# Four layers of a graph network on one core: layer 0 begins ahead of the Laplacian, its layer norm moves to GpSimd, the eigenvector chain and its products are placed anew

## The chip, the core and the metric

The kernel runs on one core of one Trainium2 chip. Time is device time in microseconds (us), the median of three runs. The engines are PE (TensorE), DVE (VectorE), ACT (ScalarE), POOL (GpSimd) and SP, which issues the transfers. Each works through its own program in order; they meet through semaphores.

## The reference

x is 128 x 64 x 128 floats (8192 rows of 128), `adj` a weighted 64 x 64 adjacency matrix. Four layers follow one another, each of this form:

```python
h = jnp.maximum(_layernorm(x, axis=-1), 0.0)
x = x + _L0_gnn_ref(h, adj, ...)   # then _L1_, _L2_, _L3_ in the same way
```

Layer 0 multiplies by the normalised adjacency matrix, then by W1 (to 256), batch norm over all rows, relu, W2 (back to 128) and batch norm again. Layer 1 is two graph convolutions and then four LSTMs over windows of 1, 2, 3 and 4 nodes, one after the other:

```python
h = jax.nn.relu(jnp.einsum('ts,bsh->bth', adj, x @ Wg0 + bg0))
h = jax.nn.relu(jnp.einsum('ts,bsh->bth', adj, h @ Wg1 + bg1))
for p in range(1, MAX_SKIP + 1):
    wins = h[:, :nw * p, :].reshape(Bv * nw, p, Hd)
    last = _lstm_last(Wih[p - 1], Whh[p - 1], bih[p - 1], bhh[p - 1], wins)
    h = h.at[:, idx, :].set(last.reshape(Bv, nw, Hd))
```

Layer 2 needs the eigenvectors of the normalised Laplacian, a 64 x 64 matrix that depends on `adj` alone:

```python
_, U = jnp.linalg.eigh(L_norm)
agg = jnp.einsum('mn,bnd->bmd', U.T, features)
h = jax.nn.relu(agg @ W1 + b1)
out = h @ W2 + b2
return jnp.einsum('nm,bmd->bnd', U, out)
```

Layer 3 is three products with `adj * adj`, each with a weight matrix. The kernel's output is x after all four.

## The kernel before

x lies in SBUF (tile X) as 16 chunks of 512 columns (4 tiles of 128); chunks come in ITER = 4 groups of NK = 4. A 64-node graph fills half the partitions, so 128 x 128 matrices made of two equal blocks (BDHT, BDP, BDR and their like) do the aggregation.

**Start.** DVE builds these matrices from `adj` one `step` after the other, first BDA and BDAT, then BDHT for layer 0, then the Laplacian LS and the matrix S that is to be reduced (lines 1271 to 1284). PE waits for "S" before its first layer-0 instruction.

**Layer 0, REFLECTED = 28 steps.** The first L0_FIRST = 19 steps pass the 16 chunks through statistics, norm, aggregation (`agg`) and W1 (`w1`), one stage a step; the other 9 do W2, two chunks a step. Beside each step stands one Householder reflection of S (`reflection_beside_l0`, lines 1335 to 1381): DVE writes NI (line 1344), PE returns a row (`row_product`), DVE copies the norm (1350), POOL takes a root (1125), DVE forms vcol (1361), PE returns a product with S (`av_product`), DVE updates S (1379, 1381). DVE's layer-0 work is a generator (`beside`, `l0_first`), from which the reflection takes an instruction wherever it would wait. The layer norm of a chunk is 4 bn_stats (line 1825), 4 bn_aggr (1832) and a shift (1841) on DVE, and on POOL a scaling (1133) and a power (1135); ACT applies it (953). In step r = 2 DVE makes the matrices of layer 1 (lines 1923 to 1928).

**The LSTM, four times (i = 0 to 3).** PE runs products of 512, 336 or 256 columns for the rounds of the four LSTMs, ACT the gates, POOL the element-wise products (line 1156). Beside iteration i the first half of layer 1 for group i + 1 is done ("tasks", the table TASKS gives the round, set and half in which each product stands). The eigenvector chain goes on beside it: the remaining 34 reflections (one `av_product` each), a grid of shifts counted by sign changes in two rounds (tile Z, lines 1529 to 1590), the twist (`both_ways`), a scan over Fq, five products on EV that correct the vectors. Their products on PE are "small": `eigen_products` yields the distance to the next in units of PE work (PACE_AV, PACE_GRID and so on), `spend` counts PE's work and sends the small product when it is due. On DVE layer 1's instructions are put between those of the chain (`beside_l1`) by a model of when PE will be where (DVE_STEP, PASS, LN_STEP, SLOWED). These two orders are fixed when the program is written; at run time an engine that reaches an instruction whose semaphore is not there waits, and all behind it with it.

**The end of the LSTM.** After the eigenvectors are done (semaphore value "all", line 1749) DVE does the layer norms' statistics for the next layers (`last_stats`: 16 x 2 bn_stats, aggregations, roots by Newton steps). In the last iteration DVE, not POOL, does the element-wise products from round 6 on (line 2050). Then follow layers 2 and 3.

Line 513 is the helper for all matrix products, line 531 a transpose of the start.

## Time and profile before

| | |
|---|---|
| median of 3 runs | 926.91 us (926.87 to 927.29) |
| the profiled execution, its time | 924.75 us |
| its span | 923.0 us |
| mean granted clock of PE | 0.972 |
| PE busy | 810.1 us (88%) |
| DVE busy | 579.1 us (63%) |
| ACT busy | 507.4 us (55%) |
| POOL busy | 311.1 us (34%) |

The chain that ended last lies on PE for 50% of the span, on DVE for 16%, on ACT for 7%. In time the program is: start to 14 us, first half of layer 0 to about 117, second half to about 160, LSTM to about 633, layers 2 and 3 to 923.

A timeline row is: start us, duration us, engine, line, operation, out<-in with shapes, xcount, and in brackets the idle time of the engine just before it and what ended that. PEld is PE's loading of a weight matrix. A window row is: start:end, length, then the busy time of PE, PEld, DVE, ACT and POOL with the number of instructions, the granted clock (1.0 is 2.4 GHz, 0.5 is 1.2 GHz), the share of the DMA engines and GB/s; a window row of PE alone has one busy time. A group row by form is: line, engine, operation, xcount, busy us, mean ns, idle us before. A row of waits is: engine, what it wrote, its line, what it waited for, total us, number, longest us.

### The profile page before, as it was taken

The page shows a single profiled execution, that of the slowest core. Times are in us where ns is not written, and L with a number is a line of the kernel's source. Part 1 is how long each engine was busy: PE and PEld are TensorE (multiplying, and loading weights), DVE is VectorE, ACT ScalarE, POOL GpSimd, SP SyncE. Part 2 cuts the span into 40 slices and gives each one's busy share as a digit, 9 for nine tenths or more (in the row PEclk, how much of TensorE's full clock was granted, in tenths as well). Part 3 has the DMA queues.
Part 4 walks back from the last instruction along what each step waited for, and adds up shares of the span by engine and source line. Part 5 has one row for each costly group of instructions (what it writes and reads, how often), then busy time and mean ns, then how long its engine had stood idle before and what let it go on. Part 6 is the DMA issues. An engine that isn't in the chain of part 4 may idle for free.

```text
span 923.0 us, 15727 instructions
## 1 busy us (share of the span) xinstructions
PE 810.1 (88%) x5323; PEld 522.7 (57%) x5323; DVE 579.1 (63%) x3092; ACT 507.4 (55%) x958; POOL 311.1 (34%) x365
## 2 busy tenths in 40 slices
PE   2787598799999988998689879988899999999998
PEld 1444343654578545684356634566656756757746
DVE  5899878689777996689794986944830530510101
ACT  1566486565755727557276464585564464443531
POOL 1233211266545735557456465600230040010000
PEclk9999989699999989999899999999999999999999
DMA  8000000000000000000000000000000100100101
GB/s 359 1 1 1 1 0 1 1 0 1 0 1 1 1 0 2 1 1 0 1 0 1 1 0 1 1 1 2 2 1 1 48 2 1 48 1 1 49 0 46
DMA packets 3408, 13.48 MB, mean 15 GB/s; under 512 B 512, under 2 KB 512, under 8 KB 2688
## 3 DMA queue, kind: packets, MB, share of 16 engines
q1 hardware_dynamic: 3328, 12.48, 3.4%
q8 instruction: 42, 0.69, 0.3%
q14 instruction: 38, 0.31, 0.1%
HBM read 8.28 MB, written 4.19 MB: 14 GB/s over the span
## 4 chain that ended last, share of the span: by engine, by line
PE 50%; DVE 16%; ACT 7%; issue 2%; POOL 2%; DVEq 0%; ACTq 0%
PE PS L513 49%; ACT BIG L1041 2%; ACT T L1007 2%; POOL BIG L1156 2%; DVE X L2032 1%; ACT T L953 1%; DVE Fq L1628 1%; DVE seg L1629 1%; DVE stats L1825 1%; ACT BIG L1065 1%; PE PS L699 1%; DVE stats L1804 1%; DVE PS L1522 1%; DVE PS L1524 1%; DVE Z L1529 1%
## 5 line engine op out<-in xcount | busy, mean ns | idle before, releaser
L513 PE MATMUL PS<-BIG,wts 128*128 128x512 f32 (+2 forms) x952 | 339.8, 499 | 10.4 <-ACT BIG L1041 8.0
L1156 POOL TENSOR_TENSOR BIG<-BIG 128x256 f32<-128x256 f32 (+2 forms) x220 | 211.5, 969 | 159.5 <-ACT BIG L1041 93.9
L513 PEld LDWEIGHTS PS<-BIG,wts 128*128 128x128 f32 x952 | 176.5, 192 | 132.9 <-issue 95.0
L1041 ACT ACTIVATE BIG<-PS,lbias 128x256 f32<-128x256 f32 (+2 forms) x312 | 162.2, 560 | 106.3 <-PE PS L513 104.3
L513 PE MATMUL PS<-H,wts 128*128 128x256 f32 (+2 forms) x312 | 113.3, 488 | 11.7 <-POOL H L1156 5.4
L945 ACT ACTIVATE BIG<-PS 128x1024 f32<-128x1024 f32 x64 | 64.8, 1023 | 85.4 <-PE PS L513 85.0
L513 PE MATMUL PS<-T,wts 128*128 128x512 f32 x192 | 100.9, 647 | 1.8 <-ACT T L945 1.6
L2077 DVE COPY T<-PS 128x256 f32<-128x256 f32 x32 | 12.0, 417 | 136.0 <-PE PS L513 136.0
L945 ACT ACTIVATE T<-PS 128x512 f32<-128x512 f32 (+1 forms) x96 | 48.3, 523 | 78.0 <-PE PS L513 77.7
L953 ACT ACTIVATE T<-X,shift,rstd 128x128 f32<-128x128 f32 x192 | 78.6, 483 | 18.2 <-DVE shift L1841 18.2
L513 PEld LDWEIGHTS PS<-H,wts 128*128 128x128 f32 x312 | 56.3, 193 | 45.2 <-issue 18.8
L2032 DVE TENSOR_TENSOR X<-X,PS 128x512 f32<-128x512 f32 x64 | 41.8, 679 | 63.0 <-PE PS L513 56.3
L1133 POOL TENSOR_SCALAR rstd<-mv 128x4 f32<-128x4 f32 x44 | 10.0, 228 | 208.6 <-DVE mv L1832 208.6
L1065 ACT ACTIVATE BIG<-BIG 128x512 f32<-128x512 f32 (+2 forms) x88 | 44.8, 510 | 51.7 <-POOL BIG L1156 50.1
L513 PE MATMUL PS<-wts,T 128*128 128x128 f32 (+1 forms) x384 | 61.9, 315 | 0.6 <-DVE T L2077 0.4
L513 PEld LDWEIGHTS PS<-wts,T 128*128 128x128 f32 x384 | 55.9, 194 | 8.0 <-issue 3.0
L513 PEld LDWEIGHTS PS<-wts,BIG 128*128 128x128 f32 x512 | 57.8, 192 | 1.9 <-issue 1.9
L513 PE MATMUL PS<-wts,BIG 128*128 128x128 f32 x512 | 57.8, 275 | 0.0
L513 PEld LDWEIGHTS PS<-T,wts 128*128 128x128 f32 x192 | 34.2, 197 | 32.9 <-issue 25.0
L1135 POOL TENSOR_TENSOR rstd<-rstd,cst 128x4 f32<-128x4 f32 x44 | 45.7, 1038 | 3.7
L1125 POOL TENSOR_TENSOR sc<-sc,cst 128x1 f32<-128x1 f32 x28 | 15.3, 548 | 93.4 <-DVE sc L1350 93.4
L1825 DVE BATCH_NORM_STATS2 stats<-X 128x6 f32<-128x128 f32 x208 | 46.6, 278 | 0.3
(319 smaller groups left out, 1136.5 us busy)
## 6 DMA issues: line engine op xcount, KB each, us to landing
X<-x_in SPq DMA_DIRECT2D x4, 1024.0 KB, 16.2
out<-X SPq DMA_DIRECT2D x16, 256.0 KB, 2.3
wts<-w_in SPq DMA_DIRECT2D x1, 3542.0 KB, 13.2
cst<-cst_in SPq DMA_DIRECT2D x1, 419.0 KB, 3.3
AA<-adj_in SPq DMA_DIRECT2D x2, 16.0 KB, 2.0
```

Source lines behind the costliest of these rows:

```text
L513: return nc.tensor.matmul(o, l, r, start=start, stop=stop)
L945: nc.scalar.activation(dst, src, fn, **kw).then_inc(act_done[k], 1)
L953: j = nc.scalar.activation(to[:, k, t * P:(t + 1) * P], X[:, a:a + P], ACT.Relu, bias=shifted[:, k, t:t + 1], scale=scale[:, k, t:t + 1])
L1007: j = nc.scalar.activation(T0[:, k, t * P:(t + 1) * P], X[:, a:a + P], ACT.Relu, bias=shift[:, k, t:t + 1], scale=rstd[:, k, t:t + 1])
L1041: nc.scalar.activation(LB[:, q, {"i": I_, "g": G_, "f": F_, "o": O_}[g], 0:n], PS[:, 3 * q + rank[q] % 3, 0:n], ACT.Tanh if g == "g" else ...
L1065: nc.scalar.activation(LB[:, q, I_, 0:n], LB[:, q, CELL, 0:n], ACT.Tanh).then_inc(act_set[q], 1)
L1125: return nc.gpsimd.tensor_tensor(o, ap, mh[:, 0:1] if e is None else e, ALU.pow)
L1135: nc.gpsimd.tensor_tensor(to[:, k, :], to[:, k, :], mh[:, 0:TPC], ALU.pow).then_inc(pool_done[k], 1)
L1156: nc.gpsimd.tensor_tensor(out, a, b, op).then_inc(pool_set[q], 1)
L1825: j = v.bn_stats(stats[:, k, t, :], X[:, a:a + P])
L2032: v.tensor_tensor(x, x, src, ALU.add).then_inc(dve_done[k], 1)
L2077: v.tensor_copy(*graph_half(k, 1, to, side)).then_inc(dve_done[k], 1)
```

## The change

1. Layer 0 starts before the Laplacian. PE waits for "hat" (BDHT) only. Steps are now counted by n, L0_STEPS = 28; the Laplacian stands on DVE in step 1, reflections begin at step FIRST_REFLECTED = 3. So 25 reflections are beside layer 0 and 37 beside the LSTM.
2. Layer 0's layer norm is bn_stats on DVE and then ten small operations on POOL (`whole_layer_norm`), which also write the shift; ACT waits for POOL.
3. The matrices of layer 1 and the LSTM's biases are made in step BIASES_AT = 23, in the second half.
4. Row and av products take 128 rows of S instead of 64.
5. The two long passes over Z become four quarters each (is_lt now against a tile of zeros), the reduction a tree of adds; instructions of layer 1 can stand between all of them.
6. New paces and new times in the model, and new places of `turn` and `turn_h` in TASKS.
7. `last_stats` is merged into the eigenvector chain; it begins 24 units after the last group's second aggregation.

```diff
-A_DVE = Steps(BEGUN, LN)
+A_DVE = Steps(BEGUN, ["stats"])
-A_POOL = Steps(BEGUN, LNP)
+A_POOL = Steps(BEGUN, WHOLE_LN)
...
+L0_STEPS = L0_FIRST + L0_SECOND
+FIRST_REFLECTED = 3
+REFLECTED = L0_STEPS - FIRST_REFLECTED
+BIASES_AT = L0_FIRST + 4
-PACE_AV = 6.7
-PACE_GRID = [47.0, 43.0]
-PACE_TWIST = 40.0
+PACE_AV = 5.9
+PACE_GRID = [49.0, 41.5]
+PACE_TWIST = 33.0
-SMALL = 0.5
+SMALL = 0.45
-SLOWED = 1.08
+SLOWED = 1.04
-PASS = 2.1
-LN_STEP = 0.5
+PASS = [0.45, 0.45, 0.45]
+QUARTER = NODES // 4
+LN_STEP = 0.42
+NORM_BESIDE, NORM_LASTS, LAST_NORMS = 1.4, 20.0, 24.0
...
-                mm(eb(0)[:, 0:NODES + 1 - k], S[0:NODES, k:k + 1].broadcast_to((NODES, P)),
-                   NI[0:NODES, k + 1:NODES + 2]).then_inc(hh_row, 1)
+                mm(eb(0)[:, 0:NODES + 1 - k], S[:, k:k + 1].broadcast_to((P, P)), NI[:, k + 1:NODES + 2]).then_inc(hh_row, 1)
...
-            pe.wait_ge(prep_dve, PREP["S"])
+            pe.wait_ge(prep_dve, PREP["hat"])
+            for n in range(L0_STEPS):
+                r, m = n - FIRST_REFLECTED, n - L0_FIRST
+                if n == 3:
+                    pe.wait_ge(prep_dve, PREP["S"])
+                if r >= 0:
+                    row_product(r)
...
+                if pace is not None and beside_norm():
+                    pace += NORM_BESIDE
...
+            def whole_layer_norm(i, k):
+                pool.wait_ge(dve_done[k], A_DVE.at(i, "stats"))
+                g.tensor_tensor(apart, even, odd, ALU.subtract).then_inc(pool_done[k], 1)
+                g.tensor_tensor(mean2, even, odd, ALU.add).then_inc(pool_done[k], 1)
+                g.tensor_tensor(m2, m2_even, m2_odd, ALU.add).then_inc(pool_done[k], 1)
+                see("apart")
+                g.tensor_tensor(between, apart, apart, ALU.mult).then_inc(pool_done[k], 1)
+                see("sum")
+                g.tensor_scalar(m2, m2, 1.0 / P, EPS, ALU.mult, ALU.add).then_inc(pool_done[k], 1)
+                g.tensor_scalar(mean2, mean2, -0.5, None, ALU.mult).then_inc(pool_done[k], 1)
+                see("square")
+                g.tensor_scalar(between, between, 0.25, None, ALU.mult).then_inc(pool_done[k], 1)
+                see("between")
+                g.tensor_tensor(var, m2, between, ALU.add).then_inc(pool_done[k], 1)
+                see("var")
+                g.tensor_tensor(rstd[:, k, :], var, mh[:, 0:TPC], ALU.pow).then_inc(pool_done[k], 1)
+                see("rstd")
+                g.tensor_tensor(shift[:, k, :], mean2, rstd[:, k, :], ALU.mult).then_inc(pool_done[k], 1)
...
-                    gop(v.tensor_scalar(Z[:, 0:NODES, :], Z[:, 0:NODES, :], 0.0, None, ALU.is_lt))
-                    busy(3 * PASS)
-                    gop(v.tensor_tensor(Z[:, 0:NODES - 1, :], Z[:, 0:NODES - 1, :], Z[:, 1:NODES, :], ALU.not_equal))
+                    for a in range(0, NODES, QUARTER):
+                        busy(PASS[0])
+                        gop(v.tensor_tensor(Z[:, a:a + QUARTER, :], Z[:, a:a + QUARTER, :], zeros, ALU.is_lt))
+                        gsync()
+                    for a in range(0, NODES, QUARTER):
+                        b = min(a + QUARTER, NODES - 1)
+                        busy(PASS[1])
+                        gop(v.tensor_tensor(Z[:, a:b, :], Z[:, a:b, :], Z[:, a + 1:b + 1, :], ALU.not_equal))
+                        gsync()
...
-                    gop(v.tensor_reduce(cn, Z[:, 0:NODES, :].rearrange("p i m -> p m i"), AX, ALU.add))
+                    while half > 2:
+                        half //= 2
+                        for a in range(0, half, QUARTER):
+                            b = min(a + QUARTER, half)
+                            busy(PASS[2] * (b - a) / QUARTER)
+                            gop(v.tensor_tensor(Z[:, a:b, :], Z[:, a:b, :], Z[:, half + a:half + b, :], ALU.add))
+                            gsync()
+                    gop(v.tensor_tensor(cn, Z[:, 0, :], Z[:, 1, :], ALU.add))
...
+            for n in range(L0_STEPS):
+                if n == 1:
+                    laplacian()
+                if n == BIASES_AT:
...
-                    at = [there[ITER - 2, NK - 1, "turn_h"]]
+                    at = [there[ITER - 1, NK - 1, "agg2"] + LAST_NORMS]
...
-                        yield from behind
-                        yield from last_stats()
+                        yield from merged(last_stats(), behind)
```

Three places at which instructions stand otherwise. First, DVE's program at the passes over Z in the first round of the grid (L1804 are layer 1's bn_stats). Before:

```order
L1560 TENSOR_SCALAR Z<-Z 128x2048 [waits grid_ops]
L1563 TENSOR_TENSOR Z<-Z 128x2016 [waits grid_ops]
L1804 BN_STATS stats<-X 128x6
L1565 SCALAR_TENSOR_TENSOR Z<-xg,PS 128x32 [waits grid_ops,dve_done2]
L1804 BN_STATS stats<-X 128x6
L1567 TENSOR_REDUCE counts<-Z 128x32 [waits grid_ops]
L1804 BN_STATS stats<-X 128x6
L1573 TENSOR_SCALAR tmp<-cst,counts 128x128 [waits grid_ops]
```

After (L1615 is the comparison with zero, L1620 the one with the neighbour, L1841 to L1853 roots of layer 1's norm, L2110 the add into X):

```order
L1615 TENSOR_TENSOR Z<-Z,zero 128x512 [waits grid_ops]
L1841 TENSOR_TENSOR lnv<-lnv 128x16 [waits ln_ops]
L1615 TENSOR_TENSOR Z<-Z,zero 128x512 [waits grid_ops]
L2110 TENSOR_TENSOR X<-X,PS 128x512 [waits pe_done2]
L1615 TENSOR_TENSOR Z<-Z,zero 128x512 [waits grid_ops]
L1844 TENSOR_TENSOR lnv<-lnv 128x16 [waits ln_ops]
L1615 TENSOR_TENSOR Z<-Z,zero 128x512 [waits grid_ops]
L1847 SCALAR_TENSOR_TENSOR lnv<-lnv 128x16 [waits ln_ops]
L1620 TENSOR_TENSOR Z<-Z 128x512 [waits grid_ops]
L1850 SCALAR_TENSOR_TENSOR lnv<-lnv 128x16 [waits ln_ops]
L1620 TENSOR_TENSOR Z<-Z 128x512 [waits grid_ops]
L1853 TENSOR_SCALAR rstd<-lnv 128x16 [waits ln_ops]
```

A pass is now four instructions, and layer 1's stand between them.

Second, PE's program around the second product of the grid, PS<-sc,cst, in the third iteration of the LSTM (BIG,wts are gates of the LSTM). Before:

```order
L513 MATMUL PS<-BIG,wts 128x256 [waits act_set1,pool_set1]
L513 MATMUL PS<-BIG,wts 128x256 [waits act_set1] x2
L513 MATMUL PS<-wts,T 128x128 [waits act_done2,act_done1]
L513 MATMUL PS<-wts,T 128x128 x3
L513 MATMUL PS<-sc,cst 128x1 [waits grid_cnt]
L513 MATMUL PS<-BIG,wts 128x256 [waits act_set0] x3
```

After:

```order
L525 MATMUL PS<-BIG,wts 128x256 [waits pool_set0]
L525 MATMUL PS<-BIG,wts 128x256 x2
L525 MATMUL PS<-BIG,wts 128x256 [waits act_set0]
L525 MATMUL PS<-BIG,wts 128x256
L525 MATMUL PS<-sc,cst 128x1 [waits grid_cnt]
L525 MATMUL PS<-BDR,T 128x128 [waits act_done2,dve_done1]
L525 MATMUL PS<-BDR,T 128x128 x3
```

The product now stands ahead of the second aggregation (agg2, BDR,T) of chunk 2, where it stood among the g1 products (PS<-wts,T) of the same iteration.

Third, DVE's program from the twist (both_ways) to the scan (Fq). Before:

```order
L1650 TENSOR_SCALAR both_ways<-Fq 64x64 [waits prep_dve]
L1651 TENSOR_TENSOR Fq<-Fq,Tdir 128x64 [waits prep_dve]
L1652 TENSOR_SCALAR Fq<-Fq 128x64 [waits prep_dve]
L1653 COPY both_ways<-Fq 64x64 [waits prep_dve]
L1656 TENSOR_TENSOR Fq<-PS,Fq 128x64 [waits prep_pe,prep_dve]
L1657 TENSOR_TENSOR Fq<-Fq 128x64 [waits prep_dve]
L1658 TENSOR_REDUCE sc<-Fq 128x1 [waits prep_dve]
```

After (L2066 are bn_stats of `last_stats`):

```order
L1716 TENSOR_TENSOR Fq<-Fq,Tdir 128x64 [waits prep_dve]
L1717 TENSOR_SCALAR Fq<-Fq 128x64 [waits prep_dve]
L1718 COPY both_ways<-Fq 64x64 [waits prep_dve]
L2066 BN_STATS stats<-X 128x6 [waits prep_dve]
L2066 BN_STATS stats<-X 128x6 x2
L2066 BN_STATS stats<-X 128x6 [waits dve_done1]
L2066 BN_STATS stats<-X 128x6 x2
L1721 TENSOR_TENSOR Fq<-PS,Fq 128x64 [waits prep_pe]
L2066 BN_STATS stats<-X 128x6
L1722 TENSOR_TENSOR Fq<-Fq 128x64 [waits prep_dve]
L2066 BN_STATS stats<-X 128x6 [waits dve_done2]
```

What stood behind the whole chain before stands inside it.

## Rows read from the trace of the kernel before

**Rows 1.** Windows, all engines, 245 to 340 (LSTM stage): busy us, granted clock.

```profile
245.00:340.00 95.00, 91.86 (x393) 61.15 (x391) 76.84 (x529) 53.94 (x104) 54.09 (x60) 0.98 0.00 1
```

**Rows 2.** Timeline of layer 0, DVE: start, duration, engine, line, operation.

```profile
64.29 0.23 DVE L1344 TENSOR_SCALAR NI<-cst,S 128x2 f32<-128x2 f32 x1
...
69.55 0.23 DVE L1344 TENSOR_SCALAR NI<-cst,S 128x2 f32<-128x2 f32 x1
...
101.03 0.23 DVE L1344 TENSOR_SCALAR NI<-cst,S 128x2 f32<-128x2 f32 x1
...
105.81 0.23 DVE L1344 TENSOR_SCALAR NI<-cst,S 128x2 f32<-128x2 f32 x1
```

**Rows 3.** Timeline of the start, DVE.

```profile
10.79 0.35 DVE L1269 TENSOR_SCALAR BDHT<-PS,col 128x128 f32<-128x128 f32 x1 [0.64 <-PE PS L531]
...
14.47 0.23 DVE L1344 TENSOR_SCALAR NI<-cst,S 128x2 f32<-128x2 f32 x1
...
23.70 0.28 DVE L1923 TENSOR_SCALAR tmp<-PS 128x128 f32<-128x128 f32 x1
...
26.25 0.23 DVE L1344 TENSOR_SCALAR NI<-cst,S 128x2 f32<-128x2 f32 x1
...
37.74 0.23 DVE L1344 TENSOR_SCALAR NI<-cst,S 128x2 f32<-128x2 f32 x1
```

**Rows 4.** Timeline of the second half of layer 0, PE's weight load.

```profile
132.95 0.18 PEld L513 LDWEIGHTS PS<-NI,S 64*128 64x128 f32 x1 [0.87 <-DVE NI L1344]
```

**Rows 5.** Groups by form, POOL: xcount | busy us, mean ns | idle before.

```profile
L1156 POOL TENSOR_TENSOR BIG<-BIG 128x256 f32<-128x256 f32 x82 | 58.9, 726 | 48.6 <-ACT BIG L1041 34.2 <-ACT BIG L1065 12.9
...
L1135 POOL TENSOR_TENSOR rstd<-rstd,cst 128x4 f32<-128x4 f32 x44 | 45.7, 1038 | 3.7
...
L1133 POOL TENSOR_SCALAR rstd<-mv 128x4 f32<-128x4 f32 x44 | 10.0, 228 | 208.6 <-DVE mv L1832 208.6
```

**Rows 6.** Waits of PE in 160 to 500: total, times, longest, in us.

```profile
PE PS L699 <- DVE X L2032: 7.8, 1, 7.8
PE PS L513 <- DVE S L1443: 7.0, 5, 2.2
```

**Rows 7.** Windows of PE at the lower clock (four stretches).

```profile
445.30:452.10 6.80, 3.80 (x8) 0.50 0.00 0
...
sum 17.00, PE 14.00; mean PE 3.50
```

**Rows 8.** Timeline of DVE beside the LSTM: one reflection's step, one root's operation.

```profile
225.44 1.07 DVE L1779 TENSOR_TENSOR lnv<-lnv 128x16 f32<-128x16 f32 x1
...
227.26 0.17 DVE L1779 TENSOR_TENSOR lnv<-lnv 128x16 f32<-128x16 f32 x1
...
231.93 0.27 DVE L1443 TENSOR_SCALAR S<-S,sc 128x1 f32<-128x1 f32 x1
...
236.85 0.27 DVE L1443 TENSOR_SCALAR S<-S,sc 128x1 f32<-128x1 f32 x1
```

**Rows 9.** Groups by form, DVE: the two long passes over Z.

```profile
L1567 DVE TENSOR_REDUCE counts<-Z 128x32 f32<-128x2048 f32 x2 | 7.3, 3673 | 0.0
...
L1563 DVE TENSOR_TENSOR Z<-Z 128x2016 f32<-128x2016 f32 x2 | 6.0, 3017 | 0.1
```

**Rows 10.** Timeline from the grid's second product to the twist.

```profile
505.57 0.28 PE L513 MATMUL PS<-sc,cst 128*128 128x1 f32 x2
...
521.70 1.16 PE L513 MATMUL PS<-BDR,T 128*128 128x128 f32 x8 [1.01 <-DVE T L1970]
...
550.10 0.23 DVE L1656 TENSOR_TENSOR Fq<-PS,Fq 128x64 f32<-128x64 f32 x1 [1.85 <-PE PS L513]
```

**Rows 11.** Timeline of the eigenvectors' end and DVE's first LSTM product.

```profile
578.75 0.33 PE L513 MATMUL PS<-EV,cst 64*64 64x64 f32 x2
...
586.76 0.28 DVE L1741 TENSOR_TENSOR EV<-EV,cst 64x128 f32<-64x128 f32 x1
...
600.06 0.92 DVE L2050 TENSOR_TENSOR BIG<-BIG 128x336 f32<-128x336 f32 x2
```

More of the change, by code:

```diff
@@ L174 @@
                    lambda i: of(i + 1, "norm3", "mix1T") * (i + 1 < ITER))
[L175 removed]
+D_DVE = two_layers(C_DVE.end, of(0, "half", "add_h") + of(1, "half") + of(0, "o", "add", *LN3)
                    + of(1, "o", "add") + of(0, "half3"),
@@ L675, in send, with beside_norm @@
                 clock[0] += SMALL
+                if pace is not None and beside_norm():
+                    pace += NORM_BESIDE
                 due[0] = None if pace is None else max(due[0], clock[0] - 1.0) + pace
+            def beside_norm():
+                return any((j, 1, "turn") in there and clock[0] < there.get((j, NK - 1, "turn"), clock[0]) + NORM_LASTS
+                           for j in range(1, ITER))
             def spend(us, i=None, k=None, name=None):
@@ L964, in _ @@
                     i, k = divmod(n - 1, NK)
-                    norm_tiles(i, k, "norm", A_DVE.at(i, "shift"), A_PE.start(i))
+                    norm_tiles(i, k, "norm", A_POOL.at(i, "shift"), A_PE.start(i), by=pool_done)
                 if is_chunk(n - 2):
@@ L1864, in l0_first @@
                         dve.wait_ge(act_done[k], A_ACT.at(i - 1, "norm"))
-                    yield from stats_of(i, k, A_DVE)
+                    for t in range(TPC):
+                        a = i * SG + k * CH + t * P
+                        j = v.bn_stats(stats[:, k, t, :], X[:, a:a + P])
+                        if t == TPC - 1:
+                            j.then_inc(dve_done[k], 1)
+                        yield
+                for _ in range(AFTER_STATS):
+                    yield
                 if is_chunk(n - 3):
```

144 lines of the change are left out of this document (78 added, 66 removed).

## The prediction

> **What bounds the kernel now.** I read the busy times of the stages first, then the waits of PE, then the timelines at the places that the change touches. Beside the LSTM (160 to 633 us) PE is the engine that everything else waits for: 91.86 of 95 us busy between 245 and 340 [rows 1]. There DVE's eigenvector chain costs something only where PE reaches one of its small products before DVE has delivered, or where DVE is late for an add: 7.8 us once before an add into X, 7.0 us in five waits for a reflection's S column, the longest 2.2 [rows 6]. Layer 0, before that, is a loop of DVE and PE around the reflection: a step takes 5.26 us with a layer norm in it (64.29 to 69.55) and 4.78 without one (101.03 to 105.81) [rows 2]. At the end of the LSTM the last rounds' products are DVE's own; the first starts at 600.06, only after the eigenvector chain and all of `last_stats`, so this chain sets the stage's end [rows 11]. Layers 2 and 3, from 633 on, are not touched.
>
> The sum is made against the profiled execution (924.75 us), which is 2.16 below the median of the runs (926.91).
>
> **Start of layer 0.** Before, BDHT ends at 11.14, the Laplacian follows, and reflection 0 starts at 14.47; reflections 0 to 3 then run beside a pipeline that is only filling, and reflection 4 starts at 37.74 [rows 3]. After, stats(0) come at 11.1 (-3.4), the six LSTM matrix operations (23.70 to 26.25, 2.55 us [rows 3]) are gone from the third step (-2.5), and three of the steps have no reflection. What fills the pipe instead is POOL's longer layer norm, ACT's norm, and PE's aggregation and w1: some 3 us longer than from stats to shift on DVE, but without the waits of three loops of about 4.8 us each [rows 2]. I take -1.1 for the two together (between +3 and -5). Start: -3.4 - 2.5 - 1.1 = **-7.0** (range -3 to -10).
>
> **Steps with a layer norm.** Four aggregations and the shift leave DVE in 12 steps. The step can lose between nothing (they stood in waits) and the 0.48 us by which a step with a layer norm is longer [rows 2]; the four stats stay, so I take a third, 0.17: **-2.0**. POOL now has ten small operations per chunk. Three TENSOR_SCALARs are 0.228 each, the pow 1.04 [rows 5]. The six small adds and products on 128x4 are not in the trace: at most the pow's 1.04, at least what 726 ns for 256 columns leaves, about 0.15. I take 0.25, nearest to the 0.228 row, and 0.07 between dependent ones: 0.7 + 1.0 + 1.5 + 0.7 = 3.9 us, with the reflection's own root (0.6) under 5.1, so POOL just fits the step.
>
> **LSTM matrices in the second half.** Those 2.55 us now stand in a loop in which PE waits 0.87 us for DVE's NI each step [rows 4], so they lengthen it: **+2.5** (0 if ACT hides them). Products over 128 rows instead of 64: PE's time goes by columns, 0. Layer 0 in all: -6.5.
>
> **Beside the LSTM, until the grid's second product.** The 7.8 and about 6 of the 7.0 us [rows 6] go, since the adds no longer stand behind the two long passes (3.67 and 3.02 us each [rows 9]) and the pauses near the norms are longer: -13.8. After each of those stalls PE ran at clock 0.50, that is 1.2 GHz; four such stretches, 17.0 us in which it was busy 14.0 [rows 7]. That is up to 7.0 lost; -5.0, as new stalls bring some back. New stalls: 37 reflections instead of 34 now stand closer (5.9 against 6.7 in the planner's units). A reflection's step without layer-1 work needs 4.92 us of DVE (231.93 to 236.85 [rows 8]); going through the 36 steps with the layer-1 instructions that the order puts between them (0 to 5.7 us a step, weighted 0.85), against 6.4 us of PE work on average and 4.9 at least, DVE is late in ten of them, by 0.3 to 1.4: +7.0. Around the first grid product the quarters and the add tree take as much as the passes they replace: +0.7. Together -13.8 - 5.0 + 7.7 = -11.1. In the new order the grid's second product stands right before the second aggregation (BDR,T) of chunk 2, which PE reached at 521.70 before [rows 10]; so it comes at 510.6, in before's time without layer 0's shift, and not at 505.57.
>
> **From there to DVE's LSTM products.** Before: 505.57 to 578.75, 73.2 us, to the last product on EV [rows 10, 11]. The twist's product is sent 7 units earlier, so its 1.85 us wait [rows 10] shrinks to 0.5: -1.35. Inside the scan DVE now has 9 stats, 16 aggregations, 8 root operations and an add: 33 by 0.17 [rows 8] and 0.5 for the add, +6.2 (at 0.10 each 3.8, at the disturbed 1.07 far more), in a stretch in which PE leaves it no wait. Between the EV products seven more: +1.3. The tail: 578.75 to 587.04 as before, 8.3, roots between 2.0, the four copies 1.3: 11.6 where it was 21.3 (to 600.06). Half clock in the new stalls +0.7. So 510.6 + 73.2 - 1.35 + 6.2 + 1.3 + 11.6 + 0.7 = 602.2 against 600.06: **+2.2**. The large saving before and the large saving of `last_stats` behind meet a chain that begins 5 us later and carries what was taken out behind it.
>
> Sum: -6.5 + 2.2 = -4.3, so the profiled execution at 920.4 and the median at **922.5**.
>
> **A rule weighed.** The same root operation on two SBUF inputs took 0.17 us at 227.26 and 1.07 at 225.44 [rows 8], with POOL in a long LSTM product at the second. The Trainium skill's "GPSIMD Engine Reference", Specifications, says that GpSimd's SBUF interfaces are shared with VectorE, with contention for DVE instructions that have two SBUF inputs. By that rule the trace agrees, and it speaks against this change: is_lt over Z had one input and gets a second (the zeros), and each long pass becomes pieces that can each wait for POOL. By the rule the sum would be rival E's; without it, mine.
>
> **Rivals.**
> A, faster. DVE keeps pace with the closer reflections and the scan's additions fall into its waits: no 7.0 and no 6.2, so 909.4; half of that 916. For it: DVE was busy only 76.8 of 95 us [rows 1]. Against it: the waits of PE for S at a looser pace [rows 6].
> B, slower. DVE bounds the reflections: the step needs 5.2 instead of 4.92 and layer-1 work counts in full. The same walk then gives 13.8 us of stalls instead of 7.0: 929.3. It decides from a need of about 5.2 a step; the disturbed 1.07 us in rows 8 speaks for it.
> C, slower. POOL bounds layer 0: if a small add takes over 0.34 us (at 0.45: 0.7 + 1.04 + 2.7 + 0.7 + 0.6 = 5.8 a step against 5.1), 13 steps by 0.7: +9, 931.5.
> D, the start does not do what its order says: ACT, POOL and a PE that is slow while cold fill the pipe as late as before, half of the 7.0 stays: 926.
> E, slower than my case. The pieces of the passes over Z, with two inputs each, wait for POOL's products as the operation at 225.44 did: some 15 pieces in the first round, half of which meet one and wait about 0.4 us (half of 1.07 less 0.17), in a stretch without slack: +3, 925.6. In the second round DVE has slack.
>
> **How the numbers follow.** My case 0.45 (own range 918 to 926), A 0.20, B 0.12, C 0.08, D 0.08, E 0.07. What a measurement of this kernel can tell from no change is about 0.2%, 1.85 us: faster is below 925.05, slower above 928.8. Faster: 0.40 of mine, 0.20 of A, 0.02 of D and E: 0.62. Same: 0.05 + 0.11 = 0.16. Slower: B, C and the upper ends of D and E, 0.22. The range reaches to half of A and to C: 912 to 931.
>
> **What would show it.** Layer 0: reflection 1 of the new count (the fifth step) at 30.7 in place of 37.74; steps of 5.1 with a layer norm and one of about 7.2 in the second half; POOL's ten operations in 3.9 us. Beside the LSTM: no wait before an add longer than 2 us, ten or so waits for S of 0.3 to 1.4, the grid's second product near 504 (510.6 - 6.5). DVE's first LSTM product near 596. The forecast is wrong if the reflections' waits sum to under 2 or over 12 us, if POOL's layer norm takes over 4.5, or if DVE's first LSTM product comes before 590 or after 600.

## The result, and the profile after

The changed kernel takes 898.35 us (median of 4 runs, 896.06 to 899.2) against 926.89 before: ratio 0.9688, 95% interval 0.967 to 0.9706. That is 28.5 us faster; 4.4 were forecast, and 898.35 lies outside the range of 912 to 931. The profiled execution has a span of 896.5 us, 26.5 less than before. All medians and ratios are of executions in the fast state; one execution, of e5, took 2819 us and is left out.

I lay the two traces side by side at the same matrix products, those that multiply BIG or H with a weight matrix (PS<-BIG,wts and PS<-H,wts). Both traces have 1264 of them; the first thousand or so are the LSTM's, the last ones lie in layers 2 and 3. The n-th of them starts so much earlier after the change:

```
n            0      270    330    510    570    600    780    840    900    1260
before    192.8    313.6  353.4  422.5  464.9  481.4  553.3  584.9  603.8  900.5
after     183.2    297.6  329.4  396.7  428.7  449.1  516.6  559.5  578.2  874.1
earlier     9.6     16.1   24.0   25.8   36.2   32.2   36.7   25.5   25.6   26.5
```

Three things are to be read from it. Up to the LSTM's first product it is 9.6 us. Beside the LSTM PE gains another 27, in part steadily, in part at the places where it waited before. And 11 of them are lost again between n = 780 and 840, that is from 517 to 560 us. The 9.6 is a reading of one execution: in e18, the same kernel profiled again, the first product starts at 180.8 and not at 183.2, so single profiles do not tell 2 us in layer 0 apart.

The start and the steps of layer 0, DVE, against [rows 2, 3] (the fifth step starts at 29.75, later ones are at 50.52 and 55.65, two of the second half at 142.85 and 147.16):

```profile
10.55 0.35 DVE L1316 TENSOR_SCALAR BDHT<-PS,col 128x128 f32<-128x128 f32 x1 [0.64 <-PE PS L543]
10.93 0.87 DVE L1928 BATCH_NORM_STATS2 stats<-X 128x6 f32<-128x128 f32 x4
...
16.98 0.22 DVE L1395 TENSOR_SCALAR NI<-cst,S 128x2 f32<-128x2 f32 x1
...
29.75 0.23 DVE L1395 TENSOR_SCALAR NI<-cst,S 128x2 f32<-128x2 f32 x1
```

```profile
50.52 0.23 DVE L1395 TENSOR_SCALAR NI<-cst,S 128x2 f32<-128x2 f32 x1
55.65 0.23 DVE L1395 TENSOR_SCALAR NI<-cst,S 128x2 f32<-128x2 f32 x1
```

```profile
142.85 0.23 DVE L1395 TENSOR_SCALAR NI<-cst,S 128x2 f32<-128x2 f32 x1
147.16 0.23 DVE L1395 TENSOR_SCALAR NI<-cst,S 128x2 f32<-128x2 f32 x1
```

A step of the first half takes 5.13 us (5.26 before), one of the second half 4.31 (4.63 before):

```profile
128.04 0.23 DVE L1344 TENSOR_SCALAR NI<-cst,S 128x2 f32<-128x2 f32 x1
132.67 0.23 DVE L1344 TENSOR_SCALAR NI<-cst,S 128x2 f32<-128x2 f32 x1
```

The last reflection beside layer 0 starts at 147.16, before at 155.76. The layer norm on POOL, by groups (xcount | busy us, mean ns | idle before), against [rows 5]:

```profile
L1180 POOL TENSOR_TENSOR rstd<-lnp,cst 128x4 f32<-128x4 f32 x16 | 16.6, 1039 | 1.3
...
L1174 POOL TENSOR_SCALAR lnp<-lnp 128x4 f32<-128x4 f32 x16 | 3.7, 228 | 1.3
...
L1169 POOL TENSOR_TENSOR lnp<-stats 128x4 f32<-128x4 f32 x16 | 3.3, 205 | 0.0
```

A small add takes 0.205 us (0.25 were assumed), and the ten operations of one chunk last from 47.33 to 50.44, 3.1 us, not 3.9. Between 30 and 110 us DVE waits for POOL once, for 0.5 us, so POOL does not bound the step.

Now the part beside the LSTM. These are windows of all engines over the same 480 products of the LSTM, first of before, then of after (length, busy PE, PEld, DVE, ACT, POOL, granted clock):

```profile
193.00:414.00 221.00, 208.99 (x863) 135.32 (x863) 178.34 (x1223) 132.75 (x261) 121.58 (x128) 0.98 0.00 1
```

```profile
183.20:387.90 204.70, 195.49 (x870) 133.49 (x869) 182.40 (x1284) 132.52 (x261) 122.48 (x129) 1.00 0.00 1
```

PE is idle for 9.2 us in place of 12.0, so hardly less. But it is *busy* for 13.5 us less, with the same work and a few more small products. Part of it is the clock: after has no stretch at the lower clock there, before had three of 3.4 us each, in which up to half the time is lost, by my estimate up to 5 us. The rest is in the timeline of PE around one reflection's small products, first before, then after:

```profile
223.11 1.02 PE L513 MATMUL PS<-BIG,wts 128*128 128x512 f32 x2
224.06 0.40 PE L513 MATMUL PS<-S,cst 64*128 64x27 f32 x2
224.31 0.38 PE L513 MATMUL PS<-S,vcol 64*128 64x29 f32 x2
224.62 1.13 PE L513 MATMUL PS<-BIG,wts 128*128 128x512 f32 x2
```

```profile
191.35 1.45 PE L525 MATMUL PS<-BIG,wts 128*128 128x512 f32 x3
192.63 0.38 PE L525 MATMUL PS<-S,cst 128*128 128x33 f32 x2
192.85 0.39 PE L525 MATMUL PS<-S,vcol 128*128 128x35 f32 x2
193.07 0.63 PE L714 MATMUL PS<-cst,T 128*128 128x128 f32 x4
```

Before, the last product of 512 columns starts at 223.54 and the small ones 0.52 us later; then it is 0.31 from the second pair to the next gate product. After, the same distances are 0.43 (192.20 to 192.63) and 0.22. From the large product before to the product behind the small ones it is 1.08 before and 0.87 after, and over all reflections beside the LSTM the median of this distance falls from 0.93 to 0.65 us. The small products of after even have more columns (33 and 35 for 27 and 29); what could make them shorter is "128*128" in place of "64*128", the number of rows. e5 and e6 test it.

The waits of PE in after, 150 to 610 us (total, times, longest), against [rows 6]:

```profile
PE PS L525 <- DVE both_ways L1718: 8.8, 1, 8.8
PE PS L525 <- ACT BIG L1061: 8.4, 11, 1.4
PE PS L525 <- ACT T L1027: 6.3, 2, 4.6
PE PS L525 <- POOL H L1205: 5.6, 4, 2.6
PE PS L525 <- DVE S L1416: 3.7, 1, 3.7
...
PE PS L719 <- DVE X L2110: 2.3, 2, 2.1
```

No wait for a reflection beside the LSTM is left (line 1494 is absent), and the wait of 7.8 before the add is 2.1. In their place stands one of 8.8 us for `both_ways`. (The wait of 3.7 for L1416 belongs to the last reflection beside layer 0, and before had it too.) And DVE in 160 to 640 us waited for PE in the reflections, first before, then after:

```profile
DVE sc L1456 <- PE PS L513: 38.7, 22, 4.8
```

```profile
DVE sc L1507 <- PE PS L525: 20.2, 20, 4.6
```

So DVE had 38.7 us of slack in the reflections before, and the closer pace used half of it.

The lower clock, against [rows 7]: three stretches, one behind the wait at 430, one that begins at 525.3, inside the wait of 523 to 531, and one behind the wait at 546 us.

```profile
433.00:437.00 4.00, 4.00 (x10) 2.29 (x9) 4.00 (x7) 1.62 (x3) 3.06 (x2) 0.57 0.01 2
526.00:536.00 10.00, 4.50 (x11) 2.72 (x12) 9.45 (x45) 0.00 (x0) 0.26 (x1) 0.52 0.00 0
548.50:552.00 3.50, 3.44 (x6) 1.40 (x6) 1.58 (x11) 0.69 (x1) 0.69 (x1) 0.60 0.00 0
```

The eigenvector chain from the grid's second product, against [rows 10, 11]:

```profile
489.49 0.28 PE L525 MATMUL PS<-sc,cst 128*128 128x1 f32 x2
```

```profile
531.50 0.79 PE L525 MATMUL PS<-both_ways,cst 128*128 128x128 f32 x2 [8.79 <-DVE both_ways L1718]
...
548.32 0.24 PE L590 MATMUL PS<-cst,Fq 64*64 64x64 f32 x1 [1.88 <-DVE Fq L1757]
```

```profile
563.98 0.33 PE L525 MATMUL PS<-EV,cst 64*64 64x64 f32 x2
...
573.30 0.23 DVE L1814 COPY BDUT<-PS 64x64 f32<-64x64 f32 x1
573.57 0.93 DVE L2128 TENSOR_TENSOR BIG<-BIG 128x336 f32<-128x336 f32 x2
```

DVE's first LSTM product starts at 573.57, 26.5 us earlier, and that is the whole gain of the span: 322.9 us follow it in both kernels.

### The profile page after: what moved, and what is told of

The parts are those of the page before. It is cut to its first block, busy times and chain, and to the rows that moved or that the text cites. A ratio compares the mean times of both kernels' runs of the same rounds, so it can differ in the third digit from the quotient of the medians.

```text
span 896.5 us, 15860 instructions
## 1 busy us (share of the span) xinstructions
PE 792.7 (88%) x5323; PEld 520.6 (58%) x5323; DVE 577.7 (64%) x3091; ACT 505.6 (56%) x958; POOL 330.9 (37%) x490
## 4 chain that ended last, share of the span: by engine, by line
PE 57%; DVE 26%; ACT 8%; POOL 5%; issue 3%; DMA 0%; DVEq 0%; SPq 0%; ACTq 0%; POOLq 0%
PE PS L525 56%; POOL BIG L1205 2%; ACT BIG L1061 2%; ACT T L1027 2%; DVE ST L1914 2%; DVE Fq L1693 1%; DVE seg L1694 1%; ACT T L973 1%; DVE X L2110 1%; DVE PS L1575 1%; DVE PS L1577 1%; DVE Z L1582 1%; DVE Z L1579 1%; ACT BIG L1085 1%; POOL sc L1145 1%
## 5 line engine op out<-in xcount | busy, mean ns | idle before, releaser
L525 PE MATMUL PS<-H,wts 128*128 128x256 f32 (+2 forms) x312 | 111.3, 485 | 10.8 <-POOL H L1205 5.6
L525 PE MATMUL PS<-T,wts 128*128 128x512 f32 x192 | 104.8, 670 | 2.9 <-ACT T L965 2.5
L973 ACT ACTIVATE T<-X,shift,rstd 128x128 f32<-128x128 f32 x192 | 78.6, 483 | 10.3 <-POOL shift L1182 9.5
L2110 DVE TENSOR_TENSOR X<-X,PS 128x512 f32<-128x512 f32 x64 | 41.9, 680 | 61.7 <-PE PS L525 56.1
L1153 POOL TENSOR_SCALAR rstd<-mv 128x4 f32<-128x4 f32 x28 | 6.4, 228 | 190.6 <-DVE mv L1897 190.5
L525 PEld LDWEIGHTS PS<-T,wts 128*128 128x128 f32 x192 | 36.0, 208 | 34.8 <-issue 28.1
L525 PEld LDWEIGHTS PS<-S,vcol 128*128 128x128 f32 x124 | 20.8, 201 | 30.8 <-DVE S L1416 26.9
L525 PE MATMUL PS<-S,vcol 128*128 128x64 f32 (+61 forms) x124 | 24.2, 275 | 13.2 <-DVE S L1416 13.1
```

The source lines that it names most:

```text
L525: return nc.tensor.matmul(o, l, r, start=start, stop=stop)
L973: j = nc.scalar.activation(to[:, k, t * P:(t + 1) * P], X[:, a:a + P], ACT.Relu, bias=shifted[:, k, t:t + 1], scale=scale[:, k, t:t + 1])
L2110: v.tensor_tensor(x, x, src, ALU.add).then_inc(dve_done[k], 1)
```

## The experiments

Each is timed beside the kernel before on the same chip. The changed kernel itself was 898.35 in the first comparison and 896.58 in e18; differences under 2 us from it are not told apart by these runs. Diffs named e1 to e3, e5, e7 to e12, e14 to e17 are against the changed kernel; e4, e6 and e13 against the kernel before.

**e1, the twist's product 4 units later.**

```diff
-PACE_TWIST = 33.0
+PACE_TWIST = 37.0
```

> The changed kernel with PACE_TWIST 37 in place of 33: PE sends the twist's product 4 units of its work later. In the changed kernel PE waits 8.8 us for both_ways. Theory 1 (from the grid's second product on DVE's own chain sets when its LSTM products can begin, and PE's wait is only the visible end of it): the wait falls from 8.8 to about 4.5, DVE's first LSTM product stays near 573.6, time 897 to 899, no change. Theory 2 (PE's progress sets the end, each of its waits is paid in full): the time falls by the 4 us of the wait, to about 894. Rival to both (the later product delays the scan behind it, as DVE already waits for it): slower by up to 3, 901.

904.19 us, ratio 0.9759 [0.9742, 0.9777]: slower than the changed kernel by 5.8. The wait for both_ways fell to 3.8, and still nothing was won, for the later places of all small products behind the twist made the chain end 4.7 us later (last product on EV at 568.64 in place of 563.98), and DVE's first LSTM product at 578.58. DVE now waited 3.0 and 2.7 us for PE among the EV products. Theories 1 and 2 both failed. The rival (slower by up to 3) had the direction and was too small: behind the twist the places in PE's program can delay the chain's end.

**e2, reflections 5.3 apart.**

```diff
-PACE_AV = 5.9
+PACE_AV = 5.3
```

> The changed kernel with PACE_AV 5.3 in place of 5.9: the 37 reflections stand closer, some 22 us of PE work in all, and the grid, twist and scan come as much earlier. Theory 1 (DVE's chain sets the start of its LSTM products): the chain ends 15 to 20 us earlier, PE's own progress then sets the end; as PE still waits 8.8 for both_ways, the gain is only the 1 to 3 us by which DVE's first LSTM product is late against its gates: 895 to 898. Theory of the prediction (a reflection needs 4.92 plus its layer-1 instructions, so new waits of 15 us or more appear at the reflections): slower, 905 to 913. If DVE's need is lower (mean about 5.0): waits for the S column under 4 us in sum.

907.57 us, 0.9789 [0.9764, 0.9815]. The waits of PE in 183 to 396 us:

```profile
PE PS L525 <- DVE S L1494: 9.8, 11, 1.8
```

So 5.3 is too close, by the prediction's kind of wait. The time lies in the 905 to 913 that its theory gave, but the waits are of less than its size (it would have given 15 or more). The chain came earlier and helped nothing. The shortest steps of DVE here are 4.72 and 4.73 us, below the 4.92 on which the prediction built.

**e3, reflections 5.6 apart, the twist's product 9 units later.**

```diff
-PACE_AV = 5.9
+PACE_AV = 5.6
-PACE_TWIST = 33.0
+PACE_TWIST = 42.0
```

> The changed kernel with PACE_AV 5.6 and PACE_TWIST 42: reflections 11 units of PE work earlier in all, the twist's product 9 later against the grid's. Theory 1: the chain begins 11 us earlier and ends about 10 earlier, the wait of 8.8 for both_ways is gone and the clock's fall behind it: faster by 8 to 11, 888 to 891. Theory 2 (waits are paid in full, whatever the chain does): the same 8 to 11. Theory of the prediction (reflections bound by DVE): 4 to 7 us of new waits at the reflections, 893 to 896.

899.56 us, 0.9714 [0.9678, 0.9749]: no better, and outside what all three theories said. The wait for both_ways is gone, but PE waits 5.4 us for S, 4.4 once before the add, and more for ACT and POOL. What DVE doesn't deliver earlier, PE can't gain by asking in another place.

**e4, the kernel before with the closer pace alone.**

```diff
-PACE_AV = 6.7
+PACE_AV = 5.9
```

> The kernel before with PACE_AV 5.9 in place of 6.7 and nothing else: one part of the change alone. Theory 1 (what counts is when DVE's LSTM products can begin and PE's waits): the chain ends some 25 us earlier, last_stats fall before the last rounds, DVE's first LSTM product is no longer late (2.3 us before), but the wait of 7.8 before the add and the clock's fall behind it stay or move: 921 to 926. Chain theory (the chain's length sets the end of the stage): 905 or less. Theory of the prediction (new waits at the reflections): slower, 928 to 934.

920.71 us, 0.9936 [0.9918, 0.9954], 5.7 us faster. The eight waits for S sum to 6.2 us (before: five, 7.0); on the first 300 products it is 6.1 us *later* than before, as the prediction thought of the pace; it gains at the add, where the 7.8 are gone (the long passes fall elsewhere), and at the end of the chain. Theory 1 (921 to 926) came nearest.

**e5 and e6, the rows of the small products.** e5: on the changed kernel 64 rows again; e6: on the kernel before 128 rows and nothing else (row_product, old_row and av_product alike). One of e5's three lines:

```diff
-                mm(eb(2)[:, 0:NODES - k], vcol[:, 0:1].broadcast_to((P, P)), S[:, k + 1:NODES + 1]).then_inc(hh_av, 1)
+                mm(eb(2)[:, 0:NODES - k], vcol[0:NODES, 0:1].broadcast_to((NODES, P)), S[0:NODES, k + 1:NODES + 1]).then_inc(hh_av, 1)
```

> The changed kernel with its row, old-row and av products on 64 rows again; all else stays. Theory M (a product on 64 rows between products on 128 makes PE empty and change over: around a reflection's small products PE needs 1.07 us from one gate product to the next before and 0.79 after, 0.28 a reflection): +0.28 x 37 = 10 beside the LSTM, +0.3 in each of the 6 second-half steps and 0.1 to 0.2 in the first half's, 12 to 16 in all, 910 to 914. Theory of the prediction (PE's time goes by columns, rows cost nothing): 898 to 899. Theory 1 (DVE's chain sets the LSTM products' start): under 5, since PE has 8.8 us of waiting for both_ways to give: 900 to 903.

> The kernel before with these products on 128 rows and nothing else. Theory M: 34 x 0.28 = 9.5 beside the LSTM and 3 to 5 in layer 0, where both products are in the loop of DVE and PE: 912 to 915, less if the wait before the add grows by what PE is earlier. Theory of the prediction: 926 to 927.

e5: 910.48 us, 0.981 [0.979, 0.983], slower than the changed kernel by 12.1. e6: 915.85 us, 0.9875 [0.9857, 0.9893], faster than before by 11.1. e5 lies in theory M's range, e6 0.9 us above it, and the prediction's nothing is refuted. In e5 PE is 4.1 us later when the LSTM begins and 10.8 after 480 products; its window over these products against that of after above:

```profile
187.20:398.80 211.60, 204.87 (x871) 134.39 (x870) 183.24 (x1285) 132.52 (x261) 122.58 (x130) 1.00 0.00 1
```

PE is busy 9.4 us more for the same work, at the same clock. The median distance around the small products is 0.92 in e5 and 0.65 in e6. In layer 0 the rows count in the second half alone: its steps are 4.63 in e5 and 4.31 in e6 (4.31 and 4.63 without the edit), those of the first half stay at 5.12 and 5.27.

The weight loads (PEld) show where the time goes. The same reflection, first after, then e5; the large product ahead of it starts at 187.03 and 190.83, the last small one at 187.71 and 191.71:

```profile
187.15 0.49 PEld L525 LDWEIGHTS PS<-S,cst 128*128 128x128 f32 x2 [0.36 <-DVE S L1494]
187.46 0.31 PE L525 MATMUL PS<-S,cst 128*128 128x34 f32 x2
...
187.79 0.30 PEld L525 LDWEIGHTS PS<-BIG,wts 128*128 128x128 f32 x2
187.82 0.68 PE L525 MATMUL PS<-BIG,wts 128*128 128x512 f32 x1
```

```profile
191.35 0.29 PEld L525 LDWEIGHTS PS<-S,cst 64*128 64x128 f32 x2 [0.76 <-DVE S L1494]
191.35 0.41 PE L525 MATMUL PS<-S,cst 64*128 64x34 f32 x2
...
191.91 0.30 PEld L525 LDWEIGHTS PS<-BIG,wts 128*128 128x128 f32 x2
191.91 0.70 PE L525 MATMUL PS<-BIG,wts 128*128 128x512 f32 x1
```

With 128 rows the first load for the small products begins 0.12 us after the large product does, 0.31 ahead of its own product. With 64 rows it begins only together with its own product, 0.52 after the large one. That is so at every reflection beside the LSTM: in before and e5 all 34 and 37 loads begin within 0.002 us of their product, in after and e6 33 of 37 and 28 of 34 begin at least 0.1 ahead. Start to start, the extra 0.28 us of a reflection is 0.09 before the first small product, 0.10 between its two passes and 0.09 behind the last one.

**e7, last_stats behind the chain again.**

```diff
-                        yield from merged(last_stats(), behind)
+                        yield from behind
+                        yield from last_stats()
```

> The changed kernel with last_stats behind the eigenvector chain again. Theory 1 (DVE's chain ends at 573.5, about when the gates of round 6 are there, so what is put behind it counts in full): DVE's first LSTM product 9 to 12 us later, less 2 to 3 because the scan and the EV products are lighter: 905 to 908. Rival (ACT and POOL have a store of work there): 898 to 900.

904.16 us, 0.9749 [0.9734, 0.9764]: 5.8 slower, a little less than theory 1 said (905 to 908) and far from its rival.

**e8, layer 0's norm on DVE again.**

```diff
-A_DVE = Steps(BEGUN, ["stats"])
+A_DVE = Steps(BEGUN, LN)
-A_POOL = Steps(BEGUN, WHOLE_LN)
+A_POOL = Steps(BEGUN, LNP)
...
-                    whole_layer_norm(n // NK, n % NK)
+                    layer_norm_roots(n // NK, n % NK, A_POOL, A_DVE)
```

> The changed kernel with layer 0's norm as before: 4 aggregations and the shift on DVE, two operations on POOL. Theory of the prediction: +0.17 a step in 12 steps and some in the start, +2 to +3: 900.5 to 901.5. Rival (the layer norm's time on POOL is what sets the start, and DVE's instructions stood in waits): faster by 1 to 2, 896 to 897.

901.55 us, 0.9728 [0.9707, 0.975]: 3.2 slower, as expected. The fifth step starts at 30.71 (29.75), and steps are 5.27 us.

**e9, the long passes over Z again.**

```diff
-                    for a in range(0, NODES, QUARTER):
-                        busy(PASS[0])
-                        gop(v.tensor_tensor(Z[:, a:a + QUARTER, :], Z[:, a:a + QUARTER, :], zeros, ALU.is_lt))
...
+                    gop(v.tensor_scalar(Z[:, 0:NODES, :], Z[:, 0:NODES, :], 0.0, None, ALU.is_lt))
+                    gsync()
+                    busy(3 * 2.1)
+                    gop(v.tensor_tensor(Z[:, 0:NODES - 1, :], Z[:, 0:NODES - 1, :], Z[:, 1:NODES, :], ALU.not_equal))
```

> The changed kernel with the two long passes over Z and the one reduction as before. Theory 1 (a wait before the add of 5 to 8 us comes back at the first grid round, with a stretch at the lower clock behind it, but PE already has 8.8 us of waiting for both_ways to give back): PE 6 to 10 us late behind the add, of which 0 to 6 are left at the end: 898 to 904. Theory of the prediction (the long passes' wait counts in full): 904 to 908. Rival (15 short pieces with two SBUF inputs cost more than they save): faster, 893 to 897.

898.48 us, 0.969 [0.9674, 0.9706]: the same as the changed kernel. Its waits of PE in 400 to 560:

```profile
PE PS L525 <- DVE both_ways L1706: 7.7, 1, 7.7
PE PS L719 <- DVE X L2098: 4.4, 2, 4.2
```

PE waits 2.1 us longer before the add and 1.1 less for both_ways, and after 720 products nothing is left of it. The quarters bring nothing here, though they cost nothing either. Theory 1's range holds, the prediction's (904 to 908) does not.

**e10, Laplacian and reflections from the first step.**

```diff
-FIRST_REFLECTED = 3
+FIRST_REFLECTED = 0
...
-                if n == 1:
+                if n == 0:
                     laplacian()
```

> The changed kernel with the Laplacian ahead of layer 0 and reflections from the first step, 28 beside layer 0 and 34 beside the LSTM. Theory of the prediction: the start costs +3.4 for the Laplacian and 1 to 2 for the three loops, and three reflections fewer beside the LSTM give back 3 x 0.6 us of PE's time: 901 to 903. Rival (the start is set by POOL's longer norm and a PE at half clock, whatever stands first): 896 to 898.

900.46 us, 0.972 [0.9694, 0.9746]. 2.1 slower, with intervals that overlap: the direction was expected (901 to 903), but it is not shown beyond the noise. In its profile PE is 5.3 us later when the LSTM begins and 2.1 at the end.

**e11, no pause of the reflections near a norm.**

```diff
-NORM_BESIDE, NORM_LASTS, LAST_NORMS = 1.4, 20.0, 24.0
+NORM_BESIDE, NORM_LASTS, LAST_NORMS = 0.0, 20.0, 24.0
```

> The changed kernel with NORM_BESIDE 0: the reflections near a layer norm of layer 1 are 5.9 units apart like the others, not 7.3. If the pause is what keeps PE from waiting for S there: 2 to 5 us of waits for S, all at the norms, chain 15 to 20 units earlier, which brings nothing while the twist keeps its distance: 900 to 903. If DVE has room there as well: 898.

908.27 us, 0.9805 [0.9781, 0.9829]: 9.9 slower. The waits of PE in 183 to 400:

```profile
PE PS L525 <- DVE S L1494: 10.2, 6, 2.3
```

Six waits, from 204 to 226 and from 306 to 334 us, around the roots of layer 1's norms (218 to 223 and 328 to 332). After 480 products PE is 11.2 us later than in after. The mechanism was expected, but with 2 to 5 us.

**e12, the EV products closer.**

```diff
-PACE = 3.6
+PACE = 3.1
-PACE_TWIST = 33.0
+PACE_TWIST = 35.0
```

> The changed kernel with PACE_TWIST 35 and the EV products 3.1 units apart in place of 3.6, an attempt at a better version: the twist's product 2 units later (its wait 8.8 to about 6.4), the last product on EV where it was. If PE's waits are paid in full and the EV steps have the 0.5 each to give (DVE waits 0.7 to 1.8 us for PE in four of them): 896 to 897. If DVE's chain from the twist on has nothing to give: 898 to 900.

901.64 us, 0.9732 [0.9714, 0.975]: 3.3 slower, above both ranges. PE waits 4.3 for Fq (1.9) and 4.1 once before the add (2.1); DVE had nothing to give.

**e13, the kernel before with 128 rows, pace 5.9 and the pause.**

```diff
-PACE_AV = 6.7
+PACE_AV = 5.9
...
+                if pace is not None and beside_norm():
+                    pace += NORM_BESIDE
```

> The kernel before with three parts of the change: products on 128 rows, PACE_AV 5.9, and the pause of 1.4 units near a layer norm. Theory 3 (the changeover of PE between 64 and 128 rows, and reflections that stand 5.9 apart but with room where a layer norm is, are most of the gain beside the LSTM): the 11 of the rows and, with the pause, 10 or more in place of the 5.7 that the pace alone gave: 900 to 907. Rival (the pause pays only with the changed tasks and model numbers): 909 to 912, as the two single parts together.

909.28 us, 0.9804 [0.9782, 0.9826], 18.5 below the kernel before on the same chip. The three parts give what rows and pace gave singly (11.1 and 5.7) and not much more, the rival's case. Its trace shows why: 19 to 21 us earlier at 540 to 660 products, then one wait of 10.6 us for T of layer 1 takes half of it away:

```profile
PE PS L515 <- DVE T L1978: 10.6, 1, 10.6
```

So the pause is worth 10 us in the changed order and 1.7 in the old one (18.5 less 11.1 and 5.7), less than these runs tell apart.

**e14, the LSTM matrices in step 5.**

```diff
-BIASES_AT = L0_FIRST + 4
+BIASES_AT = 5
```

> The changed kernel with the LSTM matrices made in step 5, in the first half of layer 0, in place of step 23. Theory of the prediction (they cost 2.5 us where they stand, in either half): no change, 898 to 899. Rival (in step 23 they stand in a wait): +2, 900 to 901.

896.99 us, 0.968 [0.9655, 0.9705]: no difference that can be told. In the profiles the step that holds them is 2.4 us longer than the same step without them in the second half (121.42 to 128.18, against 4.32) and 2.3 in the first (29.48 to 37.04, against 5.22). The step behind it is longer as well: in after 6.01 us (128.18 to 134.19), in e14 4.32 (126.62 to 130.94). The windows of the two, first after, then e14, differ in the granted clock:

```profile
128.20:134.20 6.00, 5.74 (x12) 2.46 (x12) 3.84 (x20) 2.09 (x3) 0.54 (x1) 0.72 0.00 0
```

```profile
126.60:131.00 4.40, 4.23 (x13) 1.89 (x12) 3.91 (x20) 4.15 (x7) 0.54 (x1) 1.00 0.00 0
```

So in step 23 the matrices take some 4.1 us of the profile. In step 5 it is 2.3 and another 0.35 in the step behind (5.66 against 5.31).

**e15, a longer pause.**

```diff
-PACE_AV = 5.9
+PACE_AV = 5.8
-NORM_BESIDE, NORM_LASTS, LAST_NORMS = 1.4, 20.0, 24.0
+NORM_BESIDE, NORM_LASTS, LAST_NORMS = 2.0, 20.0, 24.0
```

> The changed kernel with NORM_BESIDE 2.0 and PACE_AV 5.8, an attempt at a better version. If the pause of 1.4 already clears the waits for S (none over 0.1 us there), more brings nothing and the pace of 5.8 costs what 5.6 cost in part: 898 to 901. If the norms still cost DVE room: 895 to 897.

899.62 us, 0.97 [0.9674, 0.9726]: no better.

**e16, the twist's product 2 units earlier.**

```diff
-PACE_TWIST = 33.0
+PACE_TWIST = 31.0
```

> The changed kernel with PACE_TWIST 31: PE comes to the twist's product 2 units earlier, all small products behind it too. The wait for both_ways grows from 8.8 to about 11. If DVE's chain from the twist on is bound by PE's marks, as the 5.6 us lost with 37 suggest, it ends 2 us earlier: 896 to 898. If PE's longer wait is paid: 900 to 901.

897.91 us, 0.9684 [0.9661, 0.9707]: no difference. The wait for both_ways is 9.4. Earlier brings nothing, later costs (e1): 33 is at the edge.

**e17 and e18, both of the lowest together, and the changed kernel again, 5 rounds on one chip.**

```diff
-BIASES_AT = L0_FIRST + 4
+BIASES_AT = 5
-PACE_TWIST = 33.0
+PACE_TWIST = 31.0
```

> The changed kernel with the LSTM matrices in step 5 and PACE_TWIST 31, the two single changes that came out lowest, as an attempt to beat both kernels. If both are real and add up: 1.8 us below the changed kernel on the same chip, about 896.5. If they are run-to-run differences of layer 0 (its start varied by 1 to 2 us between profiles of kernels that are alike there): within 1 us of it.

> The changed kernel as it is, beside e17 on the same chip, as its measure: 897 to 899.5.

e17 895.37 us (0.9676 [0.9648, 0.9704]), e18 896.58 us (0.9674 [0.9655, 0.9694]). The two can't be told apart; no version was found that beats the changed kernel.

## Why the prediction was wrong

**Right.** The start: the fifth step at 29.75 for 30.7, layer 0's steps 5.13 for 5.1, the norm on POOL no bound. The LSTM matrices' own step at 2.4 us for 2.5 (by the profiles; the runs can't tell), though not the 1.7 us that the step behind it loses at the lower clock (e14). The waits that would go, 7.8 before the add and those for S, went. The tail behind the EV products: from 563.98 to 573.57 it is 9.6 for the 11.6 forecast and the 21.3 of before, and e7 puts the merging of last_stats at 5.8 us. By its own signs the forecast fails twice: the reflections' waits sum to 0, under 2, and DVE's first LSTM product comes before 590.

**Wrong, first: "Products over 128 rows instead of 64: PE's time goes by columns, 0."** This is the largest error. The row of PE's timeline that I priced it by had columns only; the change of rows between neighbouring products was not looked at, though the trace of before holds it at every reflection. It is worth 12.1 us taken out of the changed kernel (e5) and 11.1 put into the old one (e6), some 4 of them in layer 0 and 0.2 to 0.3 a reflection beside the LSTM. It explains the second half's steps of 4.31 for 4.63. In layer 0 it also hid an error: 8.6 us came for the 6.5 forecast, but with 64 rows (e5) the last reflection there starts at 150.94, only 4.8 before 155.76. Without the rows the 6.5 was 1.7 too much, about what the step behind the LSTM matrices loses. The Trainium skill has a rule that would have led here, in "TensorEngine Tiling (Array Packing)", Key Properties: "Mode switching requires drain: Changing tiling mode (not just tile) drains the TensorE". The page names neither a price nor a plain product on 64 rows; that such a product is a change of mode is my reading. The distances around the small products agree with it (median 0.93 and 0.65 us), and so do the weight loads, which begin early only between products on the same number of rows; it should have been among the rivals. That PE drains in that time is not shown; the runs show the price and that rows alone carry it.

**Wrong, second: "+7.0" for new waits at the reflections.** There were none; DVE waited for PE instead, 20.2 us in 20 waits. The 4.92 us that I took for a reflection's step without layer-1 work was too high (4.72 in e2), and DVE's slack in the reflections of before, 38.7 us, does not stand in the prediction. The prediction names the pauses near the norms as a reason why old waits go, and its walk through the steps then finds ten late ones all the same. Without the pauses there are 10.2 us of waits for S and 9.9 us more in all (e11). The mechanism exists, as e2 (9.8 us of waits at 5.3), e11 and e4 (6.2 us at 5.9 in the old order) show; at the pace and order chosen it is just not reached. With it went the stretches at the lower clock up to 388 us, which I had left standing for 2 us.

**Wrong, third: "+6.2" for the instructions in the scan.** From both_ways to Fq it is 16.8 us for 15.0 before, +1.8; that the small operations went into gaps between DVE's dependent ones is my reading. The chain from the grid's second product to DVE's first LSTM product took 84.1 us; 91.6 were forecast.

**The sum.** Against the forecast the grid's second product came at 489.5, not 504 (14.6 us), and the chain behind it was 7.5 shorter: 22.1 of the 22.2 us between -4.3 and -26.5 in the span. The first part does not come out of the named errors alone: the rows (10.8 us at n = 480 in e5), the +7.0 and the 2 us of clock, less layer 0's 1.7, make 18.1 and not 14.6. What ran 3.5 us the other way stays open.

**What the long passes did** was told wrongly too: I gave the change in them 7.8 us. With the long passes put back the time is the same (e9): the wait before the add comes back at 4.2, not at 7.8, so it was not theirs alone, and PE waits less at both_ways. Rows 9 were also misread. The 3.67 us are the reduction; the other long pass, the comparison with zero, took 1.26 and was not shown, and its four quarters now take 0.94 each (first before, then after):

```profile
L1560 DVE TENSOR_SCALAR Z<-Z 128x2048 f32<-128x2048 f32 x2 | 2.5, 1258 | 0.0
```

```profile
L1615 DVE TENSOR_TENSOR Z<-Z,zero 128x512 f32<-128x512 f32 x8 | 7.5, 938 | 0.1
```

Both passes and the reduction took DVE 8.1 us in the first round and 7.8 in the second; the pieces and the add tree take 10.3 and 12.8. So the +0.7 for the pieces was too small as work of DVE, though e9 shows no price for it.

**The rivals.** A, the faster one, named the right direction and the right absences (no new waits, the scan's additions hidden), with 909.4 at its best, and 0.20 of the chance; it lacked the rows. B, C and D did not occur. E (pieces waiting for POOL) did occur, without a price in the time: a quarter of Z takes 0.66 to 0.69 us or 1.10 to 1.27, and every one of the long ones overlaps an instruction of POOL by 0.57 us or more, though some short ones do as well. Long are one of the eight quarters in the first round and six of eight in the second. e9 has none of these pieces and the same time.

**The parts together.** e13 gives 18.5 for rows, pace and pause in the old order; with 5.8 (e7), 3.2 (e8) and 2.1 (e10) this is 29.6, against 28.5 measured. These are sums of single runs in two different kernels, and e10's is within its noise, so that they come so near is in part luck.

What stays open: why the twist's distance can't be moved either way with profit was only read from the places of the products (e1, e12, e16), and how much of the 8.8 us wait for both_ways another order could win back was not found.

## What to carry to other kernels

Look at the shape of neighbouring matrix products, not at each one's columns: a group of small products on 64 rows between products on 128 cost 0.28 us here, about 0.1 on the way in, 0.1 inside and 0.1 on the way out, and filling it up to 128 rows that add nothing to the sum was worth 11 to 12 us in this kernel. Price a term by the row and ask whether that row is undisturbed: the "free" step of 4.92 us was not. And when small work is spread beside a busy engine, try giving it room where other work is dense: the pause was worth 9.9 us in the changed order. It was worth 1.7 in the old one, so this has to be measured in the order it is meant for.
